# Taking the exponentials and feature maps of a linear-attention kernel from SBUF copies instead of from PSUM, with two buffers each

## What is computed

```python
q, k, v = x @ Wq, x @ Wk, x @ Wv            # per head, x is layer-normed
def step(carry, seg):                       # one segment of 64 rows after the other
    mem, z = carry
    sigma_q = jax.nn.elu(qq) + 1.0
    scores = where(causal, qq @ kk.T / sqrt(DK), -inf)
    att_dot = softmax(scores) @ vv
    att_mem = sigma_q @ mem / (sigma_q @ z)
    sigma_k = jax.nn.elu(kk) + 1.0
    delta = vv - sigma_k @ mem / (sigma_k @ z)
    mem_new = mem + sigma_k.T @ delta
    z_new = z + sum(sigma_k)
    att = beta * att_mem + (1 - beta) * att_dot
    out = att @ Wo
```

## Time and profile before

| | |
|---|---|
| Time, median of 3 runs | 1823.45 us (1822.89 to 1825.72) |
| The profiled execution | 1825.59 us, its span 1823.7 us |
| PE busy | 1728.6 us (95%) |
| DVE busy | 1208.0 us (66%) |
| ACT busy | 805.4 us (44%) |
| POOL busy | 916.7 us (50%) |

### The profile page before, as it was taken

The page is one execution under the profiler, slowest core; times in us unless marked ns, Lnnn a source line. Parts: engine busy times, 40 slices in busy tenths (PEclk is TensorE's granted clock), DMA queues, the critical chain, the costliest instruction groups (busy, mean ns, idle before and its releaser), DMA issues. The chain is left out here.

```text
span 1823.7 us, 45885 instructions
## 1 busy us (share of the span) xinstructions
PE 1728.6 (95%) x17990; PEld 1473.8 (81%) x17990; DVE 1208.0 (66%) x3996; ACT 805.4 (44%) x1936; POOL 916.7 (50%) x830
## 2 busy tenths in 40 slices
PE   6999999999999999999999999999999999989893
PEld 5788888888888888888888888888888888866451
DVE  6766757575767767575767677675767675663852
ACT  3544535353535445353535354453535354541040
POOL 3655646464646546464646455454646464530162
PEclk8999999999999999999999999999999999999997
DMA  4200000100000000001000000000010000046747
GB/s 152 70 22 25 15 19 8 32 8 25 15 15 25 15 25 15 19 8 32 8 22 18 15 25 15 25 15 19 8 32 8 15 25 9 25 148 188 207 80 202
DMA packets 83190, 75.23 MB, mean 41 GB/s; under 512 B 20992, under 2 KB 73808, under 8 KB 82720
## 3 DMA queue, kind: packets, MB, share of 16 engines
q1 hardware_dynamic: 79264, 65.89, 11.9%
q0 software_dynamic: 3680, 6.40, 1.9%
q10 hardware_dynamic: 32, 0.01, 0.0%
HBM read 47.78 MB, written 24.47 MB: 40 GB/s over the span
## 5 line engine op out<-in xcount | busy, mean ns | idle before, releaser
L489 POOL TENSOR_TENSOR step_place<-step_place 128x512 f32<-128x512 f32 x128 | 169.7, 1326 | 243.5 <-ACT step_place L645 243.5
L659 ACT ACTIVATE step_place<-chain_q,step_place 128x128 f32<-128x128 f32 x512 | 159.9, 366 | 275.2 <-DVE step_place L886 274.9
L902 DVE TENSOR_TENSOR step_place<-step_place,chain_k 128x258 f32<-128x258 f32 x256 | 107.7, 421 | 260.7 <-PE chain_q L1364 260.6
L525 POOL TENSOR_TENSOR step_place<-step_place 128x256 f32<-128x256 f32 x128 | 78.8, 615 | 313.5 <-DVE step_place L1079 313.5
L1410 PE MATMUL bank_o<-step_place 128*128 128x256 f32 x1024 | 226.0, 379 | 0.0
L480 POOL TENSOR_SCALAR step_place<-step_place 128x512 f32<-128x512 f32 x128 | 191.0, 1492 | 44.0 <-ACT step_place L639 43.9
L1410 PEld LDWEIGHTS bank_o<-step_place 128*128 128x128 f32 x1024 | 192.3, 190 | 25.4 <-issue 0.5
L474 POOL TENSOR_SCALAR step_place<-step_place 128x512 f32<-128x512 f32 x128 | 190.3, 1486 | 0.3 <-POOL step_place L498 0.3
L1354 PE MATMUL chain_k<-step_place 128*64 128x129 f32 x2048 | 166.0, 282 | 20.3 <-DVE step_place L902 20.2
L1364 PE MATMUL chain_k<-step_place 64*128 64x129 f32 x1024 | 181.4, 297 | 1.8 <-ACT step_place L659 1.1
L1364 PE MATMUL chain_q<-step_place 64*128 64x129 f32 x1024 | 181.6, 297 | 0.0
(11 more groups left out here) (201 smaller groups left out, 4342.1 us busy)
## 6 DMA issues: line engine op xcount, KB each, us to landing
expert_place<-in_L_ffn_w_dram SPq DMA_DIRECT2D x24, 512.0 KB, 7.8
expert_sums<-zero SPq DMA_DIRECT2D x16, 272.0 KB, 5.1
expert_rows<-w_in SPq DMA_DIRECT2D x15, 288.0 KB, 2.2
step_place<-in_L_attn_x_dram SPq DMA_DIRECT2D x16, 256.0 KB, 3.0
x_res<-in_L_attn_x_dram SPq DMA_DIRECT2D x16, 256.0 KB, 3.2
x_rows<-w_in SPq DMA_DIRECT2D x16, 256.0 KB, 2.0
x_normed_t<-x1t SPq DMA_DIRECT2D x16, 256.0 KB, 2.0
shared_place<-x_normed_t SPq DMA_DIRECT2D x8, 512.0 KB, 8.2
```

Source lines behind the costliest of these rows:

```text
L489: nc.gpsimd.tensor_tensor(vb[:, :, :, :].rearrange("p s j d -> p s (j d)"), val[:, :, :, :].rearrange("p s j d -> p s (j d)"), rows.unsque ...
L525: nc.gpsimd.tensor_tensor(sm[:, :, :], sm[:, :, :], smx[:, :].unsqueeze(2).to_broadcast([128, T, SEG]), ALU.subtract).then_inc(s["s_shifte ...
L659: ins = nc.scalar.activation(am[:, par, seg, j, :], chain_q[:, j * ZC:j * ZC + DK], ACT.Copy, scale=rdq[:, seg, j:j + 1])
L902: ins = nc.vector.tensor_tensor(m, m, (chain_k, chain_q)[b][:, 0:HG * ZC].rearrange("p (j z) -> p j z", j=HG), ALU.subtract)
```

## The change

The exponentials read the SBUF copies (`qraw`, `kraw`) instead of the PSUM banks, and each waits for the copy just before it on the same engine. They are written straight into the place of the feature maps (`sigq`, `sigk`), the minimum is taken there in place, and VectorE's feature map reads the SBUF copy as well as the capped exponential, both in SBUF, and writes over the latter. The copies get two buffers; `ex_q` and `ex_k` go; the waits of the copies and exponentials for the step before (`s_mm`, `q_sig`, `k_sig`) go. GpSimd's new helper `flat` only names the buffer.

```diff
-    qraw = take([128, HG, 2, B, SEG])
-    kraw = take([128, HG, 2, B, SEG])
-    ex_q = take([128, HG * 2 * B * SEG])
-    ex_k = take([128, HG * 2 * B * SEG])
+    qraw = take([128, 2, HG, 2, B, SEG])
+    kraw = take([128, 2, HG, 2, B, SEG])
...
+        def flat(t, n):
+
+            return t[:, n % 2, :, :, :, :].rearrange("p j s b t -> p (j s b t)")
...
-            nc.gpsimd.tensor_scalar(ex_k[:, :], ex_k[:, :], 1.0, None, ALU.min
+            nc.gpsimd.tensor_scalar(flat(sigk, n), flat(sigk, n), 1.0, None, ALU.min
                                     ).then_inc(s["k_min"], 1)
...
         def queries(n, first_ever=False):
             act.wait_ge(s["q_mm"], n + 1)
-            nc.scalar.activation(flat(qraw), bank_q[:, :], ACT.Copy).then_inc(s["q_raw"], 1)
-            if not first_ever:
-                act.wait_ge(s["q_sig"], n)
-            nc.scalar.activation(ex_q[:, :], bank_q[:, :], ACT.Exp).then_inc(s["q_exp"], 1)
+            nc.scalar.activation(flat(qraw[:, n % 2]), bank_q[:, :], ACT.Copy).then_inc(s["q_raw"], 1)
+            act.wait_ge(s["q_raw"], n + 1)
+            nc.scalar.activation(flat(sigq[:, n % 2]), flat(qraw[:, n % 2]), ACT.Exp).then_inc(s["q_exp"], 1)
 
         def keys(n, first_ever=False):
             act.wait_ge(s["k_mm"], n + 1)
-            if not first_ever:
-                act.wait_ge(s["s_mm"], n)
-            nc.scalar.activation(flat(kraw), bank_k[:, :], ACT.Copy).then_inc(s["k_raw"], 1)
-            if not first_ever:
-                act.wait_ge(s["k_sig"], n)
-            nc.scalar.activation(ex_k[:, :], bank_k[:, :], ACT.Exp).then_inc(s["k_exp"], 1)
+            nc.scalar.activation(flat(kraw[:, n % 2]), bank_k[:, :], ACT.Copy).then_inc(s["k_raw"], 1)
+            act.wait_ge(s["k_raw"], n + 1)
+            nc.scalar.activation(flat(sigk[:, n % 2]), flat(kraw[:, n % 2]), ACT.Exp).then_inc(s["k_exp"], 1)
...
         def sigma_k(n, par):
             dve.wait_ge(s["k_min"], n + 1)
             nc.vector.scalar_tensor_tensor(
                 out=sigk[:, par, :, :, :, :].rearrange("p j s b t -> p (j s b t)"),
-                in0=bank_k[:, :], scalar=0.0, in1=ex_k[:, :], op0=ALU.max, op1=ALU.add
+                in0=kraw[:, par, :, :, :, :].rearrange("p j s b t -> p (j s b t)"), scalar=0.0, in1=sigk[:, par, :, :, :, :].rearrange("p j s b t -> p (j s b t)"), op0=ALU.max, op1=ALU.add
                 ).then_inc(s["k_sig"], 1)
```

More of the change, by code:

```diff
@@ L473, in cap_queries @@
             stand_alone(pool, s["pool_noted"])
-            nc.gpsimd.tensor_scalar(ex_q[:, :], ex_q[:, :], 1.0, None, ALU.min
+            nc.gpsimd.tensor_scalar(flat(sigq, n), flat(sigq, n), 1.0, None, ALU.min
                                     ).then_inc(s["q_min"], 1)
@@ L869, in sigma_q @@
                 out=sigq[:, par, :, :, :, :].rearrange("p j s b t -> p (j s b t)"),
-                in0=bank_q[:, :], scalar=0.0, in1=ex_q[:, :], op0=ALU.max, op1=ALU.add
+                in0=qraw[:, par, :, :, :, :].rearrange("p j s b t -> p (j s b t)"), scalar=0.0, in1=sigq[:, par, :, :, :, :].rearrange("p j s b t -> p (j s b t)"), op0=ALU.max, op1=ALU.add
                 ).then_inc(s["q_sig"], 1)
@@ L1327, in scores @@
                         c = (j * B + b) * SEG
-                        ins = mm(bank_s[ROWS[seg], c:c + SEG], qraw[:, j, seg, b, :],
-                                 kraw[:, j, seg, b, :], start=True, stop=True)
+                        ins = mm(bank_s[ROWS[seg], c:c + SEG], qraw[:, n % 2, j, seg, b, :],
+                                 kraw[:, n % 2, j, seg, b, :], start=True, stop=True)
             ins.then_inc(s["s_mm"], 1)
```

## The result

| | before | changed |
|---|---|---|
| Time, median of 4 runs each | 1823.69 us (1822.89 to 1825.72) | 1926.93 us (1925.47 to 1935.05) |
| The profiled execution, and its span | 1825.59, 1823.7 | 1935.05, 1933.2 |
| Granted TensorE clock over that span | 0.987 | 0.972 |
| PE, DVE, ACT, POOL busy | 1728.6, 1208.0, 805.4, 916.7 | 1763.3, 1337.0, 848.0, 969.6 |

The changed kernel is slower by 5.7%: ratio 1.0573, with a 95% interval of 1.0543 to 1.0604. The prediction was 1895 us and a range up to 1916; the time lies above both.

A forecast was written before the change was run, and what follows sets the result against it. TensorE bounds the kernel, busy 98.94 of 100.60 us a block. GpSimd's holds on VectorE cost 1.8 + 1.4 + 0.7 + 0.8 = 4.7 us a block, 72 us in all, so 1823.45 becomes 1895 us; range 1843 to 1916.

The forecast's parts named there:

- g = 1: Loop step: keys' feature map held by GpSimd's difference, then tiny L823 held by its product; 1.8 us a block.
- g = 2: Loop step: keys' map delayed, then a Newton operation or the queries' map held by GpSimd's product; 1.4 us.
- g = 5: Loop step: queries' map and GpSimd's product arrive nearly together; 1.2 us if the product is first, else 0.25; 0.7 taken.
- g = 7: Loop step without slack: keys' map delayed, second scaling L997 held by GpSimd's product; 0.8 us.
- g = 3, 6: Loop steps: idle time and slack cover the first; a tiny operation wins back the second's loss; 0 each.
- g = 0, 4: Loop steps: slack covers VectorE's delay, with the output projection in the first; 0 each.
- block 0: First block: weight split follows the feature map in six steps; queries' minimum 0.6 us later, 0.2 hidden; 2.3 us.
- The exponential: On ScalarE: waits for its copy and reads SBUF, so ends 0.19 us later, bounds 0.11 and 0.3.
- rival 2: Feature map not held by GpSimd; only the exponential's delay counts, 3 us, so 1826 us; chance 0.11.
- The second hold at g = 2: Last Newton operation or queries' map held by GpSimd's product until 870.02; step costs 1.4 us, 0.5 without it.
- Rival 1: Keys' map held, but second meetings with GpSimd's product mostly miss; 1852 or 1877 us, range 1840 to 1880; chance 0.31.
- Rival 3: VectorE's map precedes GpSimd's difference, so L1010 slips before the product and TensorE's gap shrinks; 1813 us; chance 0.05.

The follow-up runs named there:

- the kernel with the gaps filled: Changed kernel, TensorE computing the next step's scores two or three times into the same place where it had waited; 1911.04 us.
- the edit alone on before: Kernel before the change with only its feature maps reading the SBUF copies, one buffer, exponentials still from PSUM; 1900.63 us, ratio 1.0419.
- after: The kernel with the whole change, as against the kernel before it; 1926.93 us.
- both waits: Changed kernel, GpSimd's difference waiting for the keys' feature map and its next-step product for the queries' map; 1860.83 us.
- one of them: Changed kernel with only GpSimd's difference of the values waiting for the keys' feature map; 1922.36 us, ratio 1.0538.

## Why the prediction fell short

**The cause was right.** Two inputs in SBUF make the feature map and GpSimd's operations exclude each other; with PSUM as one input nothing is left of the loss, and the same operands in the kernel before bring 76 of the 103 us. The reading of the earlier trace rows, a meeting of quite other instructions, carried over: forecast 1.7 us, measured 1.76 at g = 1 and a median of 1.685.

The Trainium skill (SBUF — State Buffer, Who interferes with whom) says that whoever issues first has the pair "for the whole instruction". The runs agree in the main and not in the last tenth: the feature map at 911.61 ended at 913.37, so its own 0.69 began 1.14 us after the start of the difference of 1.28.

**The steps,** the prediction's terms beside the measured ones:

| step | forecast us | measured us |
|---|---|---|
| g = 1 | 1.8 | 1.82 |
| g = 2 | 1.4 | 1.42 |
| g = 5 | 0.7, between 0.25 and 1.2 | 1.22 |
| g = 7 | 0.8 | 0.87 |
| g = 3, 6 | 0, 0 | 0.04, 0.07 |
| g = 0, 4 | 0, 0 | 0 |
| sum of a block | 4.7 | 5.4 |
| block 0 | 2.3 | 1.3, and 3.3 of clock |
| falls of the clock, 16 in blocks 1 to 15, together | no term | 24 |

From these, 5.44 x 15 - 0.87 is 80.7 us; with 1.3 in block 0, single steps that differ once (a wait of 1.4 in block 11, 0.4 in block 3), 0.9 at the start and -3.2 behind the loop it is 81.5; the falls, 7 of 1.50, 9 of 1.54 and 3.3, add 27.7. Together 109.2, and the profiled executions differ by 109.5. The -3.2 behind the loop is probably of this one execution and not of the change: in the kernel with the gaps filled it is -0.4.

**What failed first: the middle value at g = 5.** Both ends there stood in the working, and 0.7 was the mean of two outcomes of which only one can occur in every block, since the loop repeats to a few hundredths of a microsecond. The measured 1.22 is the upper end. The experiments show what decides: with the exponential done 0.16 us earlier (the edit alone on before) it is 0.06, with the queries' map from PSUM 0.23. The keys' map starts 0.15 us later by the exponential and with it VectorE's own queue behind it, which brings the queries' map 0.15 us behind the product; the queries' minimum is done 0.3 us before that (959.26 and 1.91 us) and does not decide here.

```profile
961.47 1.67 DVE L866 SCALAR_TENSOR_TENSOR step_place<-step_place 128x512 f32<-128x512 f32 x1 [0.15 <-DVE gsx L951]
...
961.32 1.27 POOL L491 TENSOR_TENSOR step_place<-step_place 128x512 f32<-128x512 f32 x1
```

This term is worth 0.5 x 15, 8 us.

**What failed second and weighed more: no term for TensorE's clock.** The prediction read the clock of 1.00 in the earlier trace rows as a constant and made TensorE wait, 1.7 and 1.9 us at a time, without asking what the waiting does. The falls cost some 28 us in the profiled run. In the median runs it is less: filling the gaps gave back 15.9 of the 103. With this term at 16, g = 5 at 8 more, and some 5 for the small terms (0.04 to 0.07 each in every block at g = 3, 6 and 7, the start, the wait in block 11), 1895 becomes 1924; the median was 1927. The Trainium skill (TensorE: Matmul & The Clock Gate, HAM oscillation — how this bites in real kernels) has a kernel whose TensorE falls to half the clock again and again because it stands idle between its bursts of matmuls. The runs agree in kind, with a clock of 0.50 behind gaps of 1.66 to 2.05 us; the idle stretches of the page's example are longer, and here the measurement decides.

**The upper end of the range.** It stood at 1916 because the only case above, 3 in 100, was more steps that pay. All bounds were bounds of VectorE's delay; none was of what TensorE does with it.

**The exponential.** Forecast 0.19 later, starting 0.04 behind its copy's end and taking 0.62. Measured (by shape: busy us, mean ns):

```profile
L637 ACT ACTIVATE step_place<-step_place 128x512 f32<-128x512 f32 x128 | 80.6, 630 | 4.1
```

It starts 32 ns behind the copy's end, and the minimum starts 0.175 later. But the price of rival 2, "the 0.19 counts only at g = 1: 3 us", was wrong: with the maps from PSUM the step g = 1 costs 0. The reciprocal behind the keys' map had waited 0.19 us for TensorE, and that wait, not the state addition, took the delay up; in that kernel it is gone (DVE, no idle time shown):

```profile
855.02 0.17 DVE L884 RECIPROCAL step_place<-chain_q 128x2 f32<-128x2 f32 x1
```

I had used this very cover for the feature map's delay in the sum for g = 1, and forgot it in the rival. The Trainium skill (ScalarE: Activation LUTs, What ACT_TABLE_LOAD costs) has back-to-back activations overlap by about 93 ns; the rows of before agree (0.11 us in the earlier trace rows, 103 ns in the median), and a wait on the engine's own copy turns it into a gap of 32 ns.

**The second hold at g = 2** had the right price and an open cause ("the last operation or the queries' feature map"). In after it is the former, by the kernel with only the keys' map from SBUF; in the kernel before with the maps' operands exchanged it is the latter, for 1.23 us. The expectation of the run with the keys' map alone (0.5) had settled on the latter without need.

**The rivals.** Rival 1, second meetings missed, is out: L821 took 0.97 us, as foreseen, and g = 2, 5 and 7 paid. Rival 2 is out by the durations. Rival 3's mechanism is real but never came to pass, since L500 always has a lead of at least 0.06 us over the keys' map that the same minimum releases; made by hand, it brought 14 us (1824.61 to 1810.42), where the prediction had worked out 13.

**What was to show it.** Keys' map about 1.7: yes. Queries' minimum 1.9: median 1.91. L823 about 1.0: 0.97. The queries' map at g = 2 much the same: no, it took 0.69. Gaps after g = 1, 2 and 7: yes, and also after g = 5. A block of 105 us: 106.1 in one without a fall, where the earlier trace rows has 100.6, with TensorE busy 99.60 us instead of 98.94:

```profile
905.90:1012.04 106.14, 99.60 (x1097) 87.32 (x1094) 77.29 (x237) 50.15 (x115) 57.03 (x48) 1.00 0.06 17
```

## What to carry to other kernels

Moving a VectorE operand from PSUM to SBUF costs nothing by itself and may cost as much as GpSimd's whole instruction beside it: before such a change, look for the GpSimd operation that the same semaphore releases, and for every tiny VectorE operation from SBUF to SBUF, with two inputs or a TENSOR_SCALAR with one, that a delay would push under one. Holding one engine back for the other turns holds into waits and moves the meetings: with both waits two thirds of the loss came back, with one of them 5 us of 103. Moving the operation behind the critical one, or leaving one operand in PSUM, avoids it. And where a kernel bound by TensorE gets gaps like those of 1.66 us and more here, add to the gaps what the clock takes afterwards (1.5 us for each fall, behind about half of them in after). Give a meeting that hangs on hundredths of a microsecond one of its two outcomes in the sum and both in the range.

## What the chip did that I had not expected

- TensorE's granted clock fell to 0.50 for 3.41 us behind single gaps of 1.66 to 2.05 us, each time for some 1.5 us of lost time, in some blocks and not in others that look the same. Five gaps of some 2.5 us in block 0 of one kernel brought none.
- More TensorE work made the kernel faster: repeated scores, 1926.93 to 1911.04 us.
- GpSimd's minimum, with one input, holds VectorE's small operations too, but not for its whole length. In the kernel with both waits (POOL and DVE):

```profile
888.48 1.29 POOL L502 TENSOR_TENSOR step_place<-step_place 128x512 f32<-128x512 f32 x1 [0.97 <-DVE step_place L875]
889.73 1.49 POOL L476 TENSOR_SCALAR step_place<-step_place 128x512 f32<-128x512 f32 x1
...
888.95 0.84 DVE L834 TENSOR_TENSOR a_x<-rs_x 128x2 f32<-128x2 f32 x1
889.82 0.54 DVE L835 SCALAR_TENSOR_TENSOR b_x<-a_x,v_x 128x2 f32<-128x2 f32 x1
```

  The first Newton operation lies in the difference L502 and ends with it. The second comes 0.09 us behind the start of the minimum, which runs to 891.22, and needs 0.54 us instead of 0.16, so it is held for the minimum's first 0.47 us only. The gate's product of the earlier trace rows (426 ns instead of 215), with which the prediction had put both kinds in one rule, is of this kind; the feature maps' holds are of the first.
- A VectorE operation with one input meets a second hold in the same minimum. In before the gate's L994, 168 ns when nothing holds it, comes 0.97 us behind the start of the queries' minimum and takes 0.53 us, so its own work begins 1.34 us behind that start; two-input operations that come at that point (L835 and L837 in the Newton steps) take their 0.16 us as ever.

```profile
921.91 0.53 DVE L994 TENSOR_SCALAR wsum<-wsum 128x2 f32<-128x2 f32 x1
```

- The hold by a two-input GpSimd operation has no size of its own: it lasts until that operation is nearly through. A VectorE operation of 2 values a partition is held 0.80 us (L821) and 1.01 us (L835), one of 512 for 1.07 us.
